# A graph layer on one core: the node stage's x products in split f32r, and a new order of turns on four engines

## The reference

```python
edge_index = jnp.stack([src, dst])
row, col = edge_index
h = jnp.concatenate([x[row], x[col]], axis=-1)
msgs = silu(h @ W1.T + b1) @ W2.T + b2
agg = segment_sum(msgs, row, n_nodes) / (count(row) + 1e-08)
gi = agg @ w_ih.T + b_ih
gh = x @ w_hh.T + b_hh
r, z = sigmoid(i_r + h_r), sigmoid(i_z + h_z)
n = tanh(i_n + r * h_n)
x_new = (1.0 - z) * n + z * x
g = gamma * (x_new - mean) / sqrt(var + 1e-05) + beta
out = layernorm(x + g)
```

## Time and profile before

| | us |
|---|---|
| three runs | 2466.35, 2475.81, 2476.1 (median 2475.81) |
| the profiled execution's own time | 2475.45 |
| its span | 2473.7 |
| busy: PE, DVE, ACT, POOL | 2303.0, 1994.9, 1503.2, 1420.2 |

### The profile page before, as it was taken

One profiled execution on the slowest core, in us unless ns is written; L12 is line 12 of the kernel. 1 busy time (PEld: TensorE's weight loads), 2 busy tenths in 40 slices (PEclk: granted clock), 3 DMA queues, 4 the chain that ended last, 5 costly groups with the idle time before them and its releaser, 6 DMA issues.

```text
span 2473.7 us, 46616 instructions
## 1 busy us (share of the span) xinstructions
PE 2303.0 (93%) x10226; PEld 1636.9 (66%) x10226; DVE 1994.9 (81%) x6129; ACT 1503.2 (61%) x2959; POOL 1420.2 (57%) x1479
## 2 busy tenths in 40 slices
PE   6999999999999996999899998999898999999996
PEld 4888888888888874655565555556565655655553
DVE  6777777777777764988888888888898988988888
ACT  3444444444444443766677776677676766777676
POOL 5444444444444423666666766667676766776664
PEclk9999999999999998999999999999999999999998
DMA  4666666666666655665666666666666666666663
GB/s 157 228 233 228 233 228 232 229 231 230 230 226 234 232 208 210 209 209 196 209 201 209 213 213 209 201 206 201 201 206 206 211 199 202 218 220 200 204 205 109
DMA packets 192885, 521.09 MB, mean 211 GB/s; under 512 B 51393, under 2 KB 53977, under 8 KB 192857
## 3 DMA queue, kind: packets, MB, share of 16 engines
q1 hardware_dynamic: 116752, 313.91, 35.7%
q0 software_dynamic: 75264, 206.47, 26.0%
q10 hardware_dynamic: 840, 0.40, 0.1%
HBM read 468.80 MB, written 206.73 MB: 273 GB/s over the span
## 4 chain that ended last, share of the span: by engine, by line
PE 43%; DVE 21%; issue 12%; DMA 10%; POOL 9%; ACT 2%; DVEq 2%; SPq 1%; POOLq 1%; ACTq 0%
PE banks L938 39%; DMA out_y<-yy 9%; PE banks L950 3%; POOL xb L413 3%; DVE zd L869 3%; DVE xn L875 2%; DVE rhn L852 2%; DVE st L916 2%; DVE diff L864 2%; POOL mg L347 2%; DVE tg L880 2%; POOL rs L420 2%; DVE uu L891 2%; DVE oh L843 2%; DVE ag L922 1%
## 5 line engine op out<-in xcount | busy, mean ns | idle before, releaser
L938 PE MATMUL banks<-whh,xts 128*128 128x512 f32 (+1 forms) x3136 | 1105.8, 491 | 0.0
L938 PEld LDWEIGHTS banks<-whh,xts 128*128 128x128 f32 x3136 | 558.3, 192 | 320.7 <-issue 289.9
L347 POOL DMA_INDIRECT mg<-messages,rows_now x392 | 448.3, 1144 | 170.9 <-POOL rows_now L392 77.3
L938 PE MATMUL banks<-mg,oh 128*128 128x512 f32 (+1 forms) x1568 | 336.4, 358 | 118.3 <-DVE npre L858 66.9
L413 POOL TENSOR_TENSOR xb<-xs,betab 128x512 f32<-128x512 f32 x196 | 250.4, 1278 | 319.4 <-DVE ag L922 319.4
L347 POOL DMA_INDIRECT xsrc<-in_x,src_now x196 | 187.1, 955 | 417.0 <-PE banks L950 410.0
L938 PEld LDWEIGHTS banks<-mg,oh 128*128 128x128 f32 x1568 | 263.3, 194 | 207.6 <-issue 153.1
L542 ACT ACTIVATE banks<-banks,rcount 128x768 f32<-128x768 f32 x392 | 327.5, 871 | 57.5 <-PE banks L938 43.3
L480 ACT ACTIVATE msg<-banks 128x512 fp32r<-128x512 f32 (+1 forms) x392 | 192.6, 492 | 245.3 <-PE banks L938 216.4
L564 ACT ACTIVATE yy<-uu,nm 128x256 f32<-128x256 f32 x392 | 195.6, 501 | 212.5 <-DMA out_y<-yy 209.1
L645 DVE TENSOR_TENSOR msg<-banks,msg 128x512 fp32r<-128x512 f32 (+1 forms) x392 | 200.1, 552 | 152.8 <-issue 135.0
(11 more groups left out here) (128 smaller groups left out, 4191.2 us busy)
## 6 DMA issues: line engine op xcount, KB each, us to landing
messages<-msg SPq DMA_DIRECT2D x196, 772.0 KB
xts<-in_xt SPq DMA_DIRECT2D x196, 256.0 KB
xs<-in_x SPq DMA_DIRECT2D x196, 256.0 KB
out_y<-yy SPq DMA_DIRECT2D x196, 256.0 KB
mg<-messages,rows_now POOLq DMA_INDIRECT x392
xsrc<-in_x,src_now POOLq DMA_INDIRECT x196
xdst<-in_x,dst_now POOLq DMA_INDIRECT x196
oh<-counts SPq DMA_DIRECT2D x196, 2.0 KB
```

Source lines behind the costliest of these rows:

```text
L347: nc.gpsimd.indirect_dma_start(out=dst_tile, out_offset=None, in_=rows, in_offset=bass.IndirectOffsetOnAxis(ap=table, axis=0), bounds_chec ...
L938: return nc.tensor.matmul(out_, lhsT, rhs, start=start, stop=stop, skip_group_check=skip)
```

## The change

The x products of the node stage were float32 matmuls of `xts` by `whh`. Now x is split: ACT rounds `xts` to f32r (`x_hi`, output `xh`), POOL subtracts that from `xts` (`x_lo`, output `xl`), and PE does three f32r products where there was one float32 product. `w_hh` is split once, in the preparation (`wxh` by ACT, `wxl` by DVE), and ACT waits there for DVE before it copies the biases.

Around it, the turns are ordered anew. POOL takes `rs2` for two pairs at a time. It does `x_lo` and `xb` together, from the moment at which DVE has finished `tg` (a wait on `n_tg`; before, `xb` waited for `n_a1`, the end of `ag`). DVE computes the shift `nmr` two turns later, behind `npre`, and builds `oh` behind `xn`. ACT writes the squares into `xn` instead of `yy`, and does `last_norm` (a turn later) and `squares` behind `gates1`. SP puts the store in front and loads `xts` a turn earlier.

```diff
+                hi, lo = (t[:, u, (2 * h + c) * P:(2 * h + c + 1) * P] for t in (xh, xl))
+                mm(o[:, h, 0, :], hi, wxh[:, c, 0:2 * D], False, False, True)
+                mm(o[:, h, 0, :], hi, wxl[:, c, 0:2 * D], False, False, True)
+                last = mm(o[:, h, 0, :], lo, wxh[:, c, 0:2 * D], False, c == KC - 1, True)
...
+            def x_lo(q, u):
+                if not isinstance(q, int) or q >= 5:
+                    pool.wait_ge(S["n_tg"], q - 4)
+                pool.wait_ge(S["n_xh"], q + 1)
+                need(pool, S["n_mm"], q - QU + 1)
+                nc.gpsimd.tensor_tensor(out=xl[:, u, :], in0=xts[:, u, :], in1=xh[:, u, :].bitcast(f32),
+                                        op=ALU.subtract).then_inc(S["n_xl"], 1)
...
             def add_beta(q, u):
-                pool.wait_ge(S["n_a1"], min(q + 2, PAIRS) if isinstance(q, int) else q + 2)
...
+            def x_hi(q, u):
+                act.wait_ge(got_xt[u], 16 * (nth(q, u) + 1))
+                need(act, S["n_mm"], q - QU + 1)
+                nc.scalar.activation(xh[:, u, :], xts[:, u, :], ACT.Copy).then_inc(S["n_xh"], 1)
...
-                need(act, n_stored[u], 16 * nth(q, u))
-                    last = nc.scalar.activation(yy[:, u, h * D:(h + 1) * D], uu[:, u, h * D:(h + 1) * D], ACT.Square,
+                    last = nc.scalar.activation(xn[:, u, h * D:(h + 1) * D], uu[:, u, h * D:(h + 1) * D], ACT.Square,
...
             def x_new(q, u):
+                need(dve, S["n_sq2"], q - QU + 1)
...
             def shift(q, u):
-                dve.wait_ge(S["n_r2"], q + 1)
+                dve.wait_ge(S["n_r2"], duo(q, u))
...
             def load_x(q, u):
-                need(sp, S["n_mm"], q - QU + 1)
+                need(sp, S["n_xl"], q - QU + 1)
...
-            node_turns(act, ((last_norm, -6), (tanh, -1), (gates0, 0), (mean_scale, 1), (squares, -4), (gates1, 0)), first=-1, last=7)
+            node_turns(act, ((tanh, -1), (gates0, 0), (mean_scale, 1), (x_hi, 3), (gates1, 0), (last_norm, -7), (squares, -4)), first=-3, last=7)
```

More of the change, by code:

```diff
@@ L132, in gnn_layer @@
         b2b = sb("b2b", [P, KC, P], until=setup)
-        wih = sb("wih", [P, KC, G3], until=setup)
+        wih, whh = (sb(n, [P, KC, G3], until=setup) for n in ("wih", "whh"))
         parity, place, pairi, loci = (sb(n, [P, TILES], i32, until=setup) for n in ("parity", "place", "pairi", "loci"))
@@ L148, in gnn_layer @@
         tg = sb("tg", [P, 2, 2 * D])
+        xh, xl = sb("xh", [P, QU, 2 * D], f32r), sb("xl", [P, QU, 2 * D], f32r)
         st1, ag1 = sb("st1", [P, QU, 2, 6]), sb("ag1", [P, QU, 2, 2])
@@ L341, in _ @@
             sp.wait_ge(tab_ready, 1)
-            node_turns(sp, ((load_counts, 3), (load_x, 3), (load_rows, 2), (store_y, -7)), first=-3, last=7)
+            node_turns(sp, ((store_y, -8), (load_counts, 3), (load_x, 4), (load_rows, 2)), first=-4, last=8)
             for s in range(QU):
@@ L390, in copy_rows @@
                 def copy_rows(q, u):
[L391 to L394, removed]
+                    if u % 2 == 0 and not summed:
+                        need(pool, S["n_oh"], q - QU + 2)
+                        nc.gpsimd.tensor_copy(rows_now[:, 2 * u:2 * u + 4], slot_row[:, bass.ds(2 * q, 4)])\
+                            .then_inc(idx_now, 1)
                 def gather_rows(q, u):
                     if u % 2 == 0 and not summed:
-                        copy_rows(q, u)
+                        pool.wait_ge(idx_now, 2 * E_TURNS + duo(q, u))
                     for h in range(2):
@@ L425, in inv_std2 @@
                 def inv_std2(q, u):
[L426 to L431, removed]
+                    if u % 2 == 1:
+                        pool.wait_ge(S["n_v2"], q + 1)
+                        need(pool, S["n_y"], q - QU + 1)
+                        nc.gpsimd.tensor_tensor(
+                            out=rs2[:, u - 1:u + 1, :].rearrange("p q h -> p (q h)"),
+                            in0=ve2[:, u - 1:u + 1, :].rearrange("p q h -> p (q h)"),
+                            in1=halves[:, :], op=ALU.pow).then_inc(S["n_r2"], 1)
+                node_turns(pool, ((inv_std1, -2), (inv_std2, -5), (x_lo, 2), (add_beta, -2), (gather_rows, 4), (copy_rows, 5)), first=-5, last=5)
             pool.wait_ge(ld_w, 16 * W_LOADS)
@@ L1088, in node_products @@
                 for c in range(KC):
-                    last = mm(o[:, h, 1, D:2 * D], xts[:, u, (2 * h + c) * P:(2 * h + c + 1) * P], whh[:, c, 2 * D:G3],
-                              False, c == KC - 1, True)
+                    hi, lo = (t[:, u, (2 * h + c) * P:(2 * h + c + 1) * P] for t in (xh, xl))
+                    mm(o[:, h, 1, D:2 * D], hi, wxh[:, c, 2 * D:G3], False, False, True)
+                    mm(o[:, h, 1, D:2 * D], hi, wxl[:, c, 2 * D:G3], False, False, True)
+                    last = mm(o[:, h, 1, D:2 * D], lo, wxh[:, c, 2 * D:G3], False, c == KC - 1, True)
                 return last
```

20 lines of the change are left out of this document (11 added, 9 removed).

## The result

The changed kernel takes 2442.45 us (median of four runs, 2441.13 to 2443.0) where the kernel before, run beside it, takes 2475.95 (2466.35 to 2481.56): a ratio of 0.9868, 95% interval 0.9837 to 0.9899. It is 33 us faster. That lies within the wide range given (2335 to 2455), but the forecast was 2395, 80 less than before, and the forecast's own range ended at 2415. The direction was right and six tenths of the gain are missing.

A forecast was written before the change was run, and what follows sets the result against it. PE was fullest, idling behind ACT's store wait; after the change DVE would set the turn. 196 turns of 7.19 us make 1409 instead of 1493, 84 less, plus 4 elsewhere: 2395 us, own range 2370 to 2415, wide range 2335 to 2455.

The forecast's parts named there:

- The wait on the store: ACT's wait before `squares` until `yy` was stored, 190 us in 170 turns; it was to go whole.
- Half of the x products: On PE, one half of the x products was to take 2.22 us instead of 2.70.
- The reading of the earlier trace: Behind a 3.5 us gap PE ran at its lower clock, eight matmuls taking 2.20 us instead of 1.62.
- The collision: DVE's `nmr`, `ve` and `uu` can't run beside a POOL add; `nmr` was to take 0.3 to 0.5 us.
- forecast 6.9: POOL's work per turn, 5.2 us busy before, was to be 6.9: close to a turn but not setting it.
- The floor of 6.85 us: DVE's turn if it never waited: 2.39 + 3.93 us, and 0.53 for two one-hots.
- 7.12 and 7.26: DVE's turns with POOL's adds in the way: 7.12 us, and 7.26 in every other turn, with `ve<-ag`; mean 7.19.
- where 4 was forecast: Splitting `w_hh` in the preparation, 1.6 us, and the ends of the stage, 2 to 3: together 4 us added.
- The same instructions in another order: The prediction's description of DVE's work after the change; its turn without waits was put at 6.85 us.
- The first: Rival: no collision to speak of between POOL's adds and DVE; turn 6.85 us, 2329 us; chance 0.12.
- The second: Rival: POOL, `xts` or a gather is late now and then; turn 7.4 us, 2436 us; chance 0.20.
- The fourth: Rival: `xb` gets the port before the waiting `ve<-ag`; mean turn 7.83 us, 2521 us; chance 0.08.

The follow-up runs named there:

- e2: The changed kernel with eight turns in DVE's loop instead of four: 2600.46 us, ratio 1.0507.
- e1: The kernel before with only the squares moved from `yy` into `xn`, so that they wait for no store: 2371.81 us, ratio 0.9585.
- e8: The changed kernel with POOL's wait on `tg` put last of the three waits in front of `x_lo`: 2440.11 us, ratio 0.9844.
- e6: The kernel before with the squares in `xn` and DVE's one-hots moved behind `xn`, as in the changed kernel: 2390.37 us, ratio 0.9645.
- e5: The changed kernel with DVE's one-hots back between `uu` and `nm`: 2500.36 us, ratio 1.0088.
- e12: The changed kernel with the one-hots back between `uu` and `nm` and POOL's gathers a turn earlier: 2498.32 us, ratio 1.0073.
- e3: The changed kernel without POOL's `x_lo`, the third product taking `xh` again, `xb` alone behind `tg`: 2432.41 us, ratio 0.9829.
- e4: The changed kernel's order with float32 products again, no `x_hi` or `x_lo`, `xb` behind `ag` as before: 2409.59 us, ratio 0.9739.

## Why the prediction was right and wrong

**Right.** The wait on the store is gone and no transfer took its place; the clock is 1.00. Half of the x products takes 1502.81 - 1500.59 = 2.22 us, as worked out, in these rows of PE:

```profile
1500.59 0.40 PE L959 MATMUL banks<-wxh,xh 128*128 128x512 f32 x1
...
1502.81 0.40 PE L959 MATMUL banks<-wxh,xh 128*128 128x512 f32 x1
```

DVE sets the turn. The reading of the earlier trace rows holds as well: in the trace of the kernel before the granted clock is 0.50 from 1438 to 1440 us, behind PE's gap, and 1.00 from 1441 on. The collision is there: `nmr` takes 0.32 us and ends with `xb`, `ve<-ag` 0.46, and the turn without `ve<-ag` is 7.13, forecast 7.12. POOL waits for `tg` 113.8 / 175 = 0.65 us a turn, so its own is 7.42 - 0.65 = 6.8 us, forecast 6.9.

**Wrong in size.** The step that failed is the turn of DVE. The floor of 6.85 us was read from one turn, which has no loop end, and the turns built on it, 7.12 and 7.26, have none either: 7.19 was forecast, 7.42 measured. From the first to the last `st` the 195 turns take 39.7 us less than before, where 84 was forecast; the start of the stage is 7.2 us later, where 4 was forecast (some 2 of them at the ends). What the 7.19 lacked, over four turns:

- The loop's end: 7.85 - 7.12 = 0.73 us in one turn of four, 0.18 a turn, some 35 us over the stage. By e2, 0.47 of the 0.73 go when the loop doesn't end there; the rest stays in that turn, its cause open. The earlier trace rows are the last turn of the stage, behind the loop, and no turn in them has a loop end. The kernel before has it: the medians of its four turns are 6.92, 6.99, 7.71 and 7.03 us, computed from its trace, so that it could have been read there, and e1 has it without the waiting on the store (6.85, 6.93, 7.50, 7.02). The 7.65 of the earlier trace rows against the 6.85 of the earlier trace rows was read as waiting alone; in truth 7.05 is what the old order takes without the store, and the store's damage is 0.6 us a turn.
- The turns with `ve<-ag`: 7.37 instead of 7.26, 2 x 0.11 in four turns, 11 us. In them `xl` starts 0.31 us behind `st`, not 0.16, though POOL has stood idle for 1.23 us and waits for nothing but `tg`; e8 gets some of it back by putting that wait last, so part of it lies between the wait and the add. The rest is open.

Together 0.24 us a turn in the middle, 44 us over the stage, whose first turns are shorter. The turn without `ve<-ag` came out as forecast, 7.13 for 7.12, and part of that is luck. "The same instructions in another order" says that the order costs nothing by itself, and e6 measures 18.6 us for the one-hots alone. But the turn of the earlier trace rows builds none, so its `nm` follows `uu` directly and waits the 0.12 us already, as in the new order (in the trace the read of the sum starts at 2453.20 and `nm` at 2453.32). By adding the one-hots to that turn I priced the new place without knowing it. The gap behind `st`, where `nmr` stood, costs nothing up to `rhn`: it starts 1.06 us behind `st` in the earlier trace rows and in the changed kernel.

**The rivals.** The first was refuted: it collides. The second gave the right number, 7.4 us and 2436, for a wrong reason, and so by luck: no transfer or gather is late, DVE's own turn is longer. The fourth, `xb` in front of a waiting `ve<-ag`, was given 0.08 and doesn't occur here; it occurs in e5 and e12, with 1.93 us for 0.46. What I held against it, that the waiting one goes first, goes with a quarter of a microsecond in POOL's timing. The Trainium skill (SBUF — State Buffer, Who interferes with whom) says that whoever issues first has the shared port for the whole instruction. The turn with `ve<-ag` of the changed kernel agrees, with `ve<-ag` out at the end of `xl`. In e12 it was called at 1513.12, before `xb` at 1513.77, and came out behind `xb`; here the measurement goes against the rule as I read it, and what decides is open.

**Where the expected gain went.** The squares' edit alone brings 104 us. The new order takes back 38, of which 19 for the one-hots. The products with their two adds take back 33: 10 for the second add, by e3, and 23 that lie in the turns with a held `ve<-ag`, put down to starting at `tg`. 104 - 38 - 33 = 33. The rest of the order's 38 isn't split further; the shift's place is the likeliest, and wasn't tried alone.

## What to carry to other kernels

When one wait stands in front of an instruction that an engine needs to go on, take that wait away alone first, and then ask what bounds the kernel: here everything else relieved an engine that no longer mattered and paid with the one that did. Read the floor of an engine over a whole pass of its loop, with the loop's end in it, and not from one turn that looks clean. And on an engine that is the bound, put a long independent instruction between one that makes a small result and the one that reads it.

## What the runs showed of the hardware

- The turn in which DVE's loop ends is longer than the other one without `ve<-ag`: by 0.66 us in e1, 0.73 in the changed kernel, 0.79 in e4. DVE is idle there for 0.38, 0.42 and 0.49 us. Taking the loop end out of that turn gave back 0.47 us (e2).
- A DVE loop of eight turns instead of four had 8.2 us of idle time at each pass, and 128 instead of 21 packets of instructions, three of which start in the two gaps of each pass (e2).
- DVE instructions of 128 x 2 and 128 x 4 on SBUF ended only with the POOL add that ran beside them (`nmr` 0.32 us instead of 0.15, `ve<-ag` 0.46 instead of 0.16). Which side wins between two adds in a row changed with 0.27 us in the first one's start: 0.46 against 1.93 us.
- A DVE instruction that reads what the one in front of it made starts late: `nm` 0.12 us behind the start of the accumulator's read, where an independent `oh` starts at once; `ag` after 0.15 us of idle time behind `st`.
- `rhn` and `npre`, with one operand from PSUM, kept 0.67 to 0.69 us beside both adds.
- f32r products of 512 columns follow each other at 0.23 us, of 256 at 0.12, where float32 took 2.70 us for the half that f32r does in 2.22 with three times the products.
